# Attention: where the two halves of a key tile's values stand among TensorE's products

## What is computed

```
x = x + ln(agent_attention(ln(x)))     # 0
x = x + ln(attention_and_moe(ln(x)))   # 1
x = x + ln(selective_scan(ln(x)))      # 2
x = x + ln(fp4_ffn(ln(x)))             # 3
```

```
q, k, v = (src @ Wq + bq), (src @ Wk + bk), (src @ Wv + bv)     # each as [B, T, 16 heads, 16]
scores = jnp.einsum('bqhd,bkhd->bhqk', q, k) * HEAD_DIM ** (-0.5)
probs = jax.nn.softmax(scores, axis=-1)
out = jnp.einsum('bhqk,bkhd->bqhd', probs, v)
```

## Time and profile before

| | us |
|---|---|
| median of 3 runs (3670.43 to 3679.04) | 3675.85 |
| the profiled execution | 3670.5 |
| its span, first to last instruction | 3668.8 |
| PE busy in the span | 3221.0 |
| DVE busy | 2939.5 |
| ACT busy | 2095.6 |
| head attention, first product to last values | 212.0 to 1584 |

### The profile page before, as it was taken

How to read it: one execution, slowest core, us unless ns; L and a number is a source line. 1 busy time by engine, 2 the same in 40 slices (tenths; PEclk the granted TensorE clock), 3 DMA queues, 4 the chain that set the end, 5 groups by cost and what they waited for, 6 DMA issues and landing times. The chain is left out here.

```text
span 3668.8 us, 87947 instructions
## 1 busy us (share of the span) xinstructions
PE 3221.0 (88%) x34874; PEld 1846.4 (50%) x34875; DVE 2939.5 (80%) x4783; ACT 2095.6 (57%) x2972; POOL 1198.7 (33%) x974
## 2 busy tenths in 40 slices
PE   4899999999999999973999775997899999967876
PEld 1543333333333333352666542343677787746665
DVE  5779999999999999734666254776799999948986
ACT  0317888888888888851111254666665757434553
POOL 0310000000000000025011470000899999927775
PEclk8869999999999999985999767998899999989998
DMA  1561202020202210045222263333544434231110
GB/s 58 190 173 9 38 13 45 5 46 5 45 16 56 48 25 5 6 158 188 63 64 65 74 207 121 119 124 127 147 130 120 135 107 135 78 120 52 57 35 18
DMA packets 223121, 296.00 MB, mean 81 GB/s; under 512 B 72872, under 2 KB 159536, under 8 KB 220592
## 3 DMA queue, kind: packets, MB, share of 16 engines
q1 hardware_dynamic: 211616, 264.14, 25.2%
q0 software_dynamic: 6144, 17.05, 1.4%
q10 hardware_dynamic: 5008, 9.80, 0.7%
HBM read 174.35 MB, written 115.95 MB: 79 GB/s over the span
## 5 line engine op out<-in xcount | busy, mean ns | idle before, releaser
L1016 DVE TENSOR_REDUCE att_maxima<-att_ps_m 128x1 f32<-128x512 f32 x2048 | 1274.0, 684 | 52.2 <-PE att_ps_m L1072 47.5
L971 ACT ACTIVATE att_probs<-att_ps_s 128x1024 f32<-128x1024 f32 x1024 | 1035.6, 1025 | 186.8 <-PE att_ps_s L1087 183.2
L1072 PE MATMUL att_ps_m<-held_ks,held_qs 48*128 48x512 f32 x2048 | 793.6, 465 | 5.2 <-PEq L60 4.6
L1087 PE MATMUL att_ps_s<-held_qs,held_ks 50*128 50x512 f32 x2048 | 731.6, 451 | 0.8 <-ACT att_probs L971 0.8
L1101 PE MATMUL att_ps_o<-att_probs,held_vs 128*32 128x256 f32 x8192 | 657.0, 393 | 4.7 <-ACT att_o_sb L976 0.4
L2459 POOL TENSOR_TENSOR ss_ch<-ss_h,ss_c_rep 128x1024 f32<-128x1024 f32 x256 | 601.7, 2446 | 9.1 <-DVE ss_h L2546 9.1
L1072 PEld LDWEIGHTS att_ps_m<-held_ks,held_qs 48*128 48x128 f32 x2048 | 327.3, 190 | 443.9 <-DVE att_maxima L1016 379.4
L2578 PE MATMUL ss_ps_u<-ss_diag,ss_dx_t 128*32 128x128 f32 x16384 | 475.7, 275 | 28.5 <-DMA ss_dx_t<-scratch_dx_t 14.8
L2578 PEld LDWEIGHTS ss_ps_u<-ss_diag,ss_dx_t 128*32 128x32 f32 x16384 | 454.9, 111 | 84.0 <-issue 68.1
L2498 ACT ACTIVATE ss_decay<-ss_delta,ss_a_neg 128x1024 f32<-128x1024 f32 x256 | 294.0, 1148 | 227.4 <-DVE ss_h L2546 208.0
L1101 PEld LDWEIGHTS att_ps_o<-att_probs,held_vs 128*32 128x32 f32 x8192 | 162.5, 108 | 362.7 <-ACT att_probs L971 279.2
(11 more groups left out here) (394 smaller groups left out, 4491.9 us busy)
## 6 DMA issues: line engine op xcount, KB each, us to landing
ss_delta<-scratch_delta SPq DMA_DIRECT2D x256, 128.0 KB, 3.1
held_qs<-scratch_q SPq DMA_DIRECT2D x96, 128.0 KB, 4.6
held_ks<-scratch_k SPq DMA_DIRECT2D x96, 128.0 KB, 5.1
ex_x<-scratch_sorted_x SPq DMA_DIRECT2D x72, 132.0 KB, 2.0
scratch_sorted_y<-ex_y SPq DMA_DIRECT2D x72, 128.0 KB, 1.7
scratch_q<-held_parts SPq DMA_DIRECT2D x16, 512.0 KB, 4.5
scratch_k<-held_parts SPq DMA_DIRECT2D x16, 512.0 KB, 5.2
moe_w_w<-in_W SPq DMA_DIRECT2D x16, 512.0 KB
```

The costliest lines, as they stand in the source:

```text
L971: act.activation(probs[:, (2 * n + pair) % PROBS, :, :], ps_s[pair][:, :, :], ACT.Exp, scale=HD ** -0.5).then_inc(exp_done, 1)
L1016: dve.tensor_reduce(maxima[:, j, at:at + 1], ps_m[plan.bank(key)][:, :], AX.X, ALU.max).then_inc(maxed, 1)
L1072: pe.matmul(ps_m[plan.bank(key)][:, :], qs[own, s // QC % 2, s % QC, p, t * P:(t + 1) * P], ks[own, s // QC % 2, p, c * GN:(c + 1) * GN], ...
L1087: mm = pe.matmul(ps_s[pair][:, e, :], ks[rows_of(e, 0, ROWS), st // QC % 2, pair, kt * P:(kt + 1) * P], qs[rows_of(e, 0, ROWS), st // QC % ...
```

## The change

In the loop over key tiles the first half of the values moves from the head of the key tile to a place right ahead of the second half, behind product 1. Nothing else is changed; the queues of DVE, ACT, POOL and SP are as they were.

```
                 for st in range(STEPS):
                     for kt in range(KT):
                         s, i = ahead(st, kt)
-                        last_values(st, kt, 0)
                         if s < STEPS:
                             first_pass(s, i, 0)
                         next_scores(st, kt, 0)
                         if s < STEPS:
                             first_pass(s, i, 1)
+                        last_values(st, kt, 0)
                         last_values(st, kt, 1)
                         if s < STEPS:
                             first_pass(s, i, 2)
```

## The result

The changed kernel takes 3784.88 us (median of 4 runs, 3782.39 to 3787.75) against 3673.31 us for the kernel before (4 runs): a ratio of 1.0296, 95% interval 1.0273 to 1.0318. The forecast was 3794 us and +118 us; measured are +111.6 us, inside the range of 3750 to 3860 us. The profiled executions took 3783.4 and 3670.5 us, 112.9 us apart, and this is the difference that the traces have to explain.

What follows compares the result with a forecast made beforehand. TensorE was taken to pace the kernel at 2.487 us a key tile; the ring's loop of 2.72 us adds 114.6 us over 491 key tiles, step ends 3 us: +118 us on 3675.85, 3794 us, range 3750 to 3860.

Steps and rivals of the forecast that it cites:

- The bound: Head attention before the change: TensorE sets the beat at 2.487 us a key tile; DVE is fed by it.
- The loop: Product 2's load, reduction, release, product 1's load, values, next product 2: 2.72 us a key tile, +114.6 us in all.
- the joined block: Both halves of the values in one run on TensorE: 1.01 us instead of 1.14 a key tile.
- The gap of DVE ahead of product 2's reduction: DVE idle once per key tile in the changed kernel, 0.3 us.
- The ends of the steps: Longer halves around step ends: 1.6 to 1.85 us against 1.70 before; taken as +0.1 us a step, +3 us.
- inserted tile: Turned output and turned shift, put into the ring: each makes product 1 wait one reduction later, 2 x 0.60 us.
- the copy of the output: At a step's start, values wait for ACT's copy of the old step's output; the changed kernel should lose this wait.
- third rival: TensorE's clock falls for good in the loop: about 4.2 us a key tile, +840 us, 4510 us; chance 3%.
- TensorE's saving wins: First rival: the ring does not hold product 1, DVE sets 2.40 us a key tile; -43 us, 3633 us; chance 6%.
- no difference: Second rival: the loop closes near 2.49 us, saving and wait cancel; chance within 0.2%: 4%.
- item 1: TensorE's own saving from joined values and longer product-score runs: 2.15 us a key tile instead of 2.49.
- the ring: Three banks for products: a product waits until the reduction of the product three places earlier has ended.

Runs made afterwards that it cites:

- b128: The kernel before with each maxima reduction over 128 of 512 columns; 3635.0 us, ratio to before 0.9882.
- b256: The kernel before with each maxima reduction over 256 of 512 columns; 3649.8 us, ratio to before 0.9922.
- mid: The changed kernel with the joined block of values between product 0 and scores 0 instead of behind product 1; 3900.7 us.
- a128: The changed kernel with each maxima reduction over 128 of 512 columns; 3585.6 us, ratio to before 0.9748.
- a256: The changed kernel with each maxima reduction over 256 of 512 columns; 3647.0 us, ratio to before 0.9915.
- ap3: The changed kernel without the second pair of heads' scores and exponentials, three banks in the ring; 3823.3 us.
- bp3: The kernel before without the second pair of heads' scores and exponentials, three banks in the ring; 3641.2 us.
- bp4: The kernel before without the second pair of heads' scores and exponentials, four banks in the ring; 3592.4 us.
- ap4: The changed kernel without the second pair of heads' scores and exponentials, four banks in the ring; 3624.7 us.
- head: The changed kernel with the joined block of values ahead of product 0 instead of behind product 1; 3765.1 us, ratio to before 1.0241.

## Why the prediction was right, and where its sizes were off

**The bound.** That the kernel before is paced by TensorE and not by DVE, which its busy share of 97% suggests, held: b128 does with reductions of 0.29 us what b256 and the original do, 2.48 us a key tile.

**The loop.** Forecast 0.54 + 0.69 + 0.06 + 0.42 + 1.01 = 2.72 us, measured 0.54 + 0.69 + 0.05 + 0.42 + 1.00 = 2.70, with 2.705 as the mean over longer stretches. The term on which the bounds hung, the joined block, came out within 0.01 us of what was taken. The beat of before, 2.487, was read from three halves; 18 halves from 650.00 to 672.32 us in the same trace give 2.480. So the loop costs 2.705 - 2.480 = 0.225, times 491 = 110 us instead of 114.6: 7 us too much from rounding two terms upwards, 3 too little from the beat of before. The gap of DVE ahead of product 2's reduction was forecast at 0.3 us and is 0.21 ([0.21 <-PE] above): four reductions with a gap before them take 3 x 0.60 + 0.69 = 2.49 us, not 2.39.

**The ends of the steps.** Forecast +0.1 us each, measured more. The blocks of the changed kernel around a turned shift and at the next step's start (the window cuts the last row, as it does mid's above):

```profile
...
703.78 0.59 PEld L1101 LDWEIGHTS att_ps_o<-att_probs,held_vs 128*32 128x32 f32 x16 [0.25 <-issue]
...
707.15 0.59 PEld L1101 LDWEIGHTS att_ps_o<-att_probs,held_vs 128*32 128x32 f32 x16 [0.25 <-issue]
...
717.97 0.59 PEld L1101 LDWEIGHTS att_ps_o<-att_probs,held_vs 128*32 128x32 f32 x16 [0.24 <-issue]
...
720.67 0.19 PEld L1087 LDWEIGHTS att_ps_s<-held_qs,held_ks 50*128 50x128 f32 x2 [1.15 <-ACT att_probs L971]
...
721.33 0.59 PEld L1101 LDWEIGHTS att_ps_o<-att_probs,held_vs 128*32 128x32 f32 x16 [0.36 <-issue]
...
724.64 0.37 PEld L1101 LDWEIGHTS att_ps_o<-att_probs,held_vs 128*32 128x32 f32 x12 [0.24 <-issue]
```

3.37, 3.36 and 3.31 us, together 1.93 us above three calm key tiles, against 1.72 before (a step of 41.42 less 16 key tiles of 2.481): +0.21, or some 6 us over 31 steps instead of 3. The terms were right in kind: one reduction later behind each inserted tile, 0.60 forecast and 0.60 and 0.67 measured; and 0.65 at the step's start, where scores 0 wait for an exponential (the row of L1087), the top of the 0.4 to 0.65 estimated. But the sum of 1.93 lies above the range of 1.6 to 1.85. The wait for the copy of the output did go, as said, but bought nothing, since the exponential behind that copy is later and scores 0 wait for it ahead of the values.

**The clock.** The third rival was given 3% for the whole loop, and did not come about. But at the loop's start the clock did matter, the other way, and the forecast had no term for it. The windows view from 268 to 281.5 us, before and then changed (the figure behind POOL's count, 0.50 and 0.88, is the granted clock):

```profile
...
268.00:281.50 13.50, 13.50 (x80) 4.24 (x72) 8.33 (x13) 6.17 (x7) 0.00 (x0) 0.50 1.18 133
...
```

```profile
...
268.00:281.50 13.50, 13.20 (x116) 6.19 (x113) 11.21 (x19) 8.73 (x10) 0.00 (x0) 0.88 1.18 133
...
```

The kernel before ran its first three key tiles at 1.2 GHz; their halves are 2.16 us apart in these rows, 4.33 a key tile:

```profile
...
269.68 0.20 PEld L1101 LDWEIGHTS att_ps_o<-att_probs,held_vs 128*32 128x32 f32 x8 [0.65 <-issue]
...
271.84 0.20 PEld L1101 LDWEIGHTS att_ps_o<-att_probs,held_vs 128*32 128x32 f32 x8 [0.65 <-issue]
...
```

A mean of 0.88 over 13.5 us is the full 2.4 GHz from about 271 us on; the changed kernel gained about 5 us by it. 110 + 6 - 5 = 111 of 112.9 us; the other 2 are spread over the last step, the first values and what follows the stage. So the forecast of +118 met +111.6 with the mechanism right, while the loop was taken 4 us too high, the steps' ends 3 too low, and the 5 of the clock not at all. The last 21 key tiles, without products, took 44 us, nearly as long as before (43).

**The rivals.** "TensorE's saving wins" needed a loop 0.23 us shorter; a128, where the reduction is 0.40 us shorter, is faster than b128. Near "no difference" lies a256, which takes as long as b256. In the changed kernel itself both are excluded by the same row, the 0.69 us of a reduction. That TensorE alone would need 2.15 us, the sum of item 1, no run shows: the shortest calm key tile of the joined order with all its work is the 2.30 us of a128, and there the ring binds.

## What to carry to other kernels

When work is regrouped on an in-order queue, write down for each ring of buffers the distance between the instruction that fills a buffer and the one that waits for it, in time and not in instructions: filling, draining, release, and the block that stands behind the waiting instruction form a loop, and its length is a floor for the beat that no busy share shows. Work that seemed to interrupt a stream may be what covers such a wait, here one half of the values between product 2 and the product 1 that takes its bank, with 0.07 us to spare. And a joined block is worth joining where the drain is short enough, as in a128, and not merely where the loop has ceased to bind: with a fourth bank DVE's beat took over, and the joined order was still 32 us slower than the other. Test the sign by shortening the drain.

## What the runs showed of the hardware that was not expected

- The granted clock at the loop's start differs between kernels whose products ahead of it are the same: it was 1.2 GHz for 17 whole key tiles in ap3, 13 in bp3, 8 in mid, 3 in the kernel before, b256 and bp4, one in b128, and for less than one in the changed kernel (both profiles), a256, a128, ap4 and head. In ap3 it cost 23 us in the first step; a few later steps had a short stretch at half clock too, 2 us each. The windows view of ap3's first step:

```profile
...
272.00:338.00 66.00, 65.05 (x348) 26.56 (x341) 38.91 (x65) 16.26 (x18) 0.45 (x1) 0.50 0.25 25
...
```

  A key tile of ap3 at half clock took 4.17 us, close to the 4.2 us that the third rival had been priced at, but with half of the scores left out (mid, with all the work in another order, took 4.59 us):

```profile
...
300.17 0.20 PEld L1100 LDWEIGHTS att_ps_o<-att_probs,held_vs 128*32 128x32 f32 x8 [0.44 <-issue]
...
304.34 0.20 PEld L1100 LDWEIGHTS att_ps_o<-att_probs,held_vs 128*32 128x32 f32 x8 [0.44 <-issue]
...
```

  What decides when the clock rises was not tried.
- The idle time before a product's load, put down to DVE in the rows (0.41 us in the earlier trace rows), is no wait for DVE where it reads 0.41: the same 0.41 stands before the product behind a block in b128, where the bank of the product at 717.73, whose row stands above, had been reduced by 716.4 us. By the rows it falls in the time in which the values' matmuls still run, whose loads are over: the row of 642.76 in the earlier trace rows has the loads end after 0.16 us and the matmuls, by their modelled ends, after 0.64. A real wait of product 1 shows as 0.51 or 0.52 in the changed kernel, in the same column.
